# Splitting and testing feed-forward weights on GpSimd inside the attention batches, three chunks of gates ahead of the feed-forward layers, and more bias copies by VectorE in the last batch

## The chip, the cores and the metric

One core of one Trainium2 chip. The metric is the time of the device in microseconds (us); the kernel before takes 326.47 us, the median of 3 runs (325.59 to 327.27).

## The reference, cut to what matters

A transformer block on x of 8 batches x 256 tokens x 128, all in float32: an attention with 16 heads of 8 and a bias that depends on the relative position, then a gated feed-forward part with a hidden size of 512.

```python
def attn(x):                      # x: 8 x 256 x 128
    q, k, v = split(x @ W_qkv + b_qkv)                    # 16 heads of 8
    scores = einsum('bihd,bjhd->bhij', q, k) / sqrt(8) + bias[rel]
    out = einsum('bhij,bjhd->bihd', softmax(scores), v)
    return out @ W_out + b_out
def ffn(x):                       # tlin(x, w, s) = (x @ w.T) * s
    h = silu(tlin(x, w1, s1)) * tlin(x, w2, s2)           # 128 -> 512, "gate"
    h = gelu(tlin(h, h1, s1h))                            # 512 -> 512, "layer 1"
    h = gelu(tlin(h, h2, s2h))                            # 512 -> 512, "layer 2"
    return tlin(h, w3, s3)                                # 512 -> 128, "layer 3"
x = x + layernorm(attn(layernorm(x)))
x = x + layernorm(ffn(layernorm(x)))
```

## The kernel before, in words

Five engines each run a program of their own, written out by hand in the order of the work; `wait_ge` and `then_inc` on semaphores are all that ties them together. An engine takes its instructions in order, so a wait holds back all that is behind it.

**Numbers.** float32 products are made of two halves: a value is rounded to the `float32r` type that TensorE multiplies fast (the "high" part), and the rest (the "low" part) is kept beside it. So each activation of the feed-forward part is cast (ScalarE, L994 and L1028) and subtracted (GpSimd L544 or VectorE L767, L776), and `product` (L1335, L1336) multiplies the high weights with the high and the low part. The weights themselves are split too: `w_hi` and `w_lo`, 5632 columns, in 11 pieces of 512. If every low weight is zero (here the weights are -1, 0 or 1), the program takes the branch `ffn(exact=True)` with two matmuls per product; if not, the other with four. The test for that is part of the kernel: a maximum over each piece (L714), one over the eleven (L756), a transposition on TensorE (L1329), a maximum of the row (L758), and `value_load` and `If` on TensorE.

**Attention.** Batches 0 to 7, each with 8 pairs of heads (`s` = 0 to 7). While the scores of batch b are computed, TensorE also computes those of batch b+1 for their maxima (L1144, L1154), which VectorE takes (L643); the last batch has none of that. A pair's scores (L1180) are added in PSUM to its position bias, which is copied there before by ScalarE (`write_bias`, L923) or by VectorE (L650, pairs 2 and 5), or is added by TensorE (L1191, pair 7). ScalarE takes the exponential (L916), TensorE multiplies with v (`weighted`, L1204). Three PSUM tiles take turns for the scores, so the bias of pair i waits in the last batch for the exponential of pair i-3. In batch b the steps behind the attention of batch b-1 are mixed in: `back`, `weigh`, `heads_T`, `project`, `attn_moments`, `residual`, `second_norm`, `norm_T`, `keep_zT` and `z_low`. GpSimd computes the inverse deviations (`inv_std`, L503), two for each batch, and little else.

**In the last batch** ScalarE casts the weights' eleven pieces (`weights_high`, L941, `HIGH_AT`), GpSimd subtracts seven of them (L536), VectorE four (L711), and VectorE takes all the maxima.

**Feed-forward.** Four chunks of 512 tokens. `gate(c, k)` makes one of four outputs of chunk c in two PSUM banks (`GBANK`, two pairs of banks that alternate); ScalarE takes the SiLU (L1000), VectorE the product (L785). `layer1`, `layer2` give four outputs each, 8 matmuls an output, with a GELU on ScalarE (L1026); `layer3` goes back to 128. The order on TensorE is written out in `ffn`:

```python
whole(gate, 0); back(7, 0); gates 1.0, 1.1; layer1(0) with gates 1.2, 1.3; heads_T; layer1(1)
project; layer2(0); norm_T(7); gates 2.0, 2.1; layer2(1) with gates 2.2, 2.3
layer3(0); gates 3.0, 3.1; tokens_back(0); layer1(2) with gates 3.2, 3.3; layer3(1); layer1(3) ...
```

ScalarE's order is `gates(0)`, `gates(1)`, `layer(0, 0)`, `keep_onT`, `layer(1, 0)`, `layer(0, 1)`, `keep_zT`, `gates(2)`, `layer(1, 1)`, `keep_y3T(0)`, `gates(3)`, ... (its second argument is 0 for layer 1 and 1 for layer 2). SiLU and GELU need different tables, and going from one to the other inserts a table load. `A1_BANK`, `A2_BANK`, `G_SLOT` and their like say which bank and which buffer each output has, and the `free` tables in `layer1` and `layer2` what TensorE has to wait for.

## Time and profile before

| what | value |
|---|---|
| time, median of 3 runs | 326.47 us (325.59 to 327.27) |
| time of the profiled execution | 327.04 us |
| its span, first to last instruction | 325.2 us |
| busy: TensorE, VectorE, ScalarE, GpSimd | 283.9, 217.7, 212.3, 45.2 us |
| mean granted TensorE clock | 0.900 |
| first product of the feed-forward part | 215.46 us |

The span is 1.84 us shorter than that execution's time. Times in the rows are counted from the span's first instruction. "PE" is TensorE's matmuls, "PEld" its weight loads, "DVE" VectorE, "ACT" ScalarE, "POOL" GpSimd. A row's bracket says how long the engine sat idle before it, and what released it. The granted clock is a share of 2.4 GHz: 0.50 is 1.2 GHz.

### The profile page before, as it was taken

To read this page: it belongs to the slowest core of one execution; us is meant where nothing else is said; L and a number is where in the kernel's file an instruction comes from. 1 tells how busy PE (TensorE), PEld (TensorE's weight loads), DVE (VectorE), ACT (ScalarE), POOL (GpSimd) and SP (SyncE) were. 2 spreads that over 40 slices of the span, in tenths; PEclk is the share of its full clock that TensorE was granted. 3 is DMA by queue.
4 is the path that set the end of the run, shared out by engine and by line. 5 is a ranking of instruction groups with operands and counts; after the bars stand their busy time and mean duration, and the time that the engine had idled before them with its cause. 6 is when DMAs were issued, how large, how long until landed. Compare 5 with 4: busy or idle time off the path is not lost.

```text
span 325.2 us, 5036 instructions
## 1 busy us (share of the span) xinstructions
PE 283.9 (87%) x1844; PEld 186.9 (57%) x1844; DVE 217.7 (67%) x451; ACT 212.3 (65%) x313; POOL 45.2 (14%) x52
## 2 busy tenths in 40 slices
PE   8859699989999999999999966789997979699980
PEld 7644363646565555555555533346885758488870
DVE  3855355888789788897888956936558343554485
ACT  2431246678786787857878599547796576767750
POOL 3200400000001001010010137203202110300111
PEclk9985558999999999999999997559999798989997
DMA  6889800533031254522212000000000000010012
GB/s 160 260 248 245 283 2 24 183 109 100 27 89 54 67 194 171 174 87 67 78 31 62 1 3 0 1 0 2 1 2 0 0 0 0 2 32 0 1 35 69
DMA packets 22748, 23.29 MB, mean 72 GB/s; under 512 B 3745, under 2 KB 19905, under 8 KB 22465
## 3 DMA queue, kind: packets, MB, share of 16 engines
q1 hardware_dynamic: 21872, 22.38, 23.5%
q10 hardware_dynamic: 848, 0.54, 0.6%
q8 instruction: 17, 0.28, 0.4%
q14 instruction: 11, 0.08, 0.1%
HBM read 15.93 MB, written 6.68 MB: 70 GB/s over the span
## 4 chain that ended last, share of the span: by engine, by line
PE 52%; DVE 16%; ACT 11%; DMA 8%; issue 6%; SPq 4%; POOL 1%; ACTq 0%; POOLq 0%
PE place L1335 9%; PE place L1336 9%; PE place L1154 8%; PE pv L1204 7%; DVE mx L643 6%; ACT ring L916 5%; PE place L1144 4%; PE place L1180 3%; SPq L429 3%; DMA raw<-ext 2%; PE pv L1335 2%; DVE stats L569 2%; PE pv L1336 2%; DMA k_first<-z_parts 2%; DMA k_parts<-z_parts 2%
## 5 line engine op out<-in xcount | busy, mean ns | idle before, releaser
L643 DVE TENSOR_REDUCE mx<-place 128x4 f32<-128x1024 f32 x64 | 78.3, 1223 | 26.9 <-PE place L1154 25.7
L916 ACT ACTIVATE ring<-place 128x1024 f32<-128x1024 f32 x64 | 65.6, 1026 | 7.8 <-PE place L1191 5.7
L1154 PE MATMUL place<-room,identr 128*128 128x512 f32 x128 | 52.2, 492 | 3.6 <-ACT room L882 3.1
L923 ACT COPY place<-raw 128x1024 f32<-128x1024 f32 x40 | 40.8, 1021 | 16.0 <-DVE mx L643 16.0
L503 POOL TENSOR_TENSOR rstd<-mv,mhalf 128x2 f32<-128x2 f32 (+1 forms) x26 | 21.5, 827 | 205.4 <-DVE mv L577 205.4
L1335 PE MATMUL place<-room,w_hi 128*128 128x512 f32 (+1 forms) x108 | 42.6, 397 | 3.6 <-ACT ring L1026 2.9
L1336 PE MATMUL place<-room,w_hi 128*128 128x512 f32 (+1 forms) x108 | 41.9, 391 | 0.0
L1204 PE MATMUL pv<-ring,vx 128*9 128x256 f32 x512 | 37.0, 411 | 2.0 <-ACT ring L916 1.9
L1144 PE MATMUL place<-room 33*128 33x256 f32 x256 | 31.3, 325 | 8.4 <-ACT ring L916 4.0
L1180 PE MATMUL place<-room 33*128 33x256 f32 x256 | 34.2, 348 | 4.8 <-ACT place L923 3.3
L767 DVE TENSOR_TENSOR room<-ring,room 128x512 fp32r<-128x512 f32 x32 | 21.9, 691 | 22.7 <-ACT room L1028 22.7
L1180 PEld LDWEIGHTS place<-room 33*128 33x128 f32 x256 | 20.6, 198 | 21.3 <-issue 17.0
L1144 PEld LDWEIGHTS place<-room 33*128 33x128 f32 x256 | 22.1, 207 | 16.4 <-issue 13.4
L1154 PEld LDWEIGHTS place<-room,identr 128*128 128x128 f32 x128 | 21.3, 209 | 13.4 <-ACT room L882 3.7
L1335 PEld LDWEIGHTS place<-room,w_hi 128*128 128x128 f32 x108 | 20.8, 192 | 8.3 <-ACT ring L1026 3.3
L785 DVE SCALAR_TENSOR_TENSOR ring<-place,hs,raw 128x512 f32<-128x512 f32 x16 | 11.8, 750 | 20.2 <-ACT raw L1000 20.2
L928 ACT COPY oT<-pv 128x256 f32<-128x256 f32 x32 | 11.8, 369 | 19.7 <-PE pv L1204 19.7
L1204 PEld LDWEIGHTS pv<-ring,vx 128*9 128x9 f32 x512 | 11.3, 93 | 21.4 <-issue 10.0
L1336 PEld LDWEIGHTS place<-room,w_hi 128*128 128x128 f32 x108 | 20.9, 193 | 4.0
L1026 ACT ACTIVATE ring<-place,hs 128x512 f32<-128x512 f32 x25 | 17.2, 688 | 8.3 <-PE place L1336 8.3
L1028 ACT CAST room<-ring 128x512 fp32r<-128x512 f32 x32 | 19.8, 620 | 1.0
L650 DVE COPY place<-raw 128x1024 f32<-128x1024 f32 x16 | 19.6, 1226 | 0.6
(129 smaller groups left out, 395.7 us busy)
## 6 DMA issues: line engine op xcount, KB each, us to landing
raw<-ext SPq DMA_DIRECT2D x8, 384.0 KB, 7.3
room<-q_parts SPq DMA_DIRECT2D x48, 64.0 KB
room<-k_parts SPq DMA_DIRECT2D x48, 64.0 KB
w_lo<-h SPq DMA_DIRECT2D x2, 1024.0 KB, 5.0
q_parts<-w_hi SPq DMA_DIRECT2D x4, 256.0 KB, 3.1
k_parts<-w_hi SPq DMA_DIRECT2D x2, 512.0 KB, 3.4
xs<-x SPq DMA_DIRECT2D x3, 256.0 KB, 6.3
w_lo<-w SPq DMA_DIRECT2D x3, 256.0 KB, 2.8
```

What stands on the lines that cost most here:

```text
L503: nc.gpsimd.tensor_tensor(rstd[:, at:at + width], mv[:, at:at + width, 1], mhalf[:, 0:width], ALU.pow).then_inc(rstd_set, 1)
L643: nc.vector.tensor_reduce(mx[:, s // RPAIRS, :, :, s % RPAIRS].rearrange("p i k -> p k i"), max_tile(b * PAIRS + s)[:, :, :].rearrange("p ...
L767: nc.vector.tensor_tensor(lo, act_f[:, half[c], k, :], hi.bitcast(F32), ALU.subtract).then_inc((a1_lo_set, a2_lo_set)[i], 1)
L916: nc.scalar.activation(probs[:, s % PRING, :, :, :].rearrange("p k j n -> p (k j n)"), score_tile(b * PAIRS + s)[:, :, :].rearrange("p k n ...
L923: nc.scalar.copy(score_tile(i)[:, :, :].rearrange("p k (j n) -> p k j n", j=2), pair_windows(raw[:, :, :], i % PAIRS)).then_inc(bias_set, 1)
L1028: nc.scalar.copy(parts_of(slot[c], k)[0], tile).then_inc(hi_set, 1)
L1144: mm(max_tile(b * PAIRS + s)[:, half, it * S:(it + 1) * S], rows(q_rows, b, half, s)[:, it * P:(it + 1) * P], rows(k_rows, b, half, s), st ...
L1154: last = mm(max_tile(b * PAIRS + s)[:, half, :], identr[:, :], windows(table_hi[:, 2 * s + half, :], 0, P, 2, S), start=False, stop=True, ...
L1180: last = mm(tile[:, half, j * S:(j + 1) * S], rows(k_rows, b, half, s)[:, j * P:(j + 1) * P], rows(q_rows, b, half, s), start=(s in BY_PE ...
L1204: last = mm(pv[32 * r:32 * r + VC, 0:S], vx[:, b * TPB + j, 4 * g + r, :], probs[:, (2 * g + r // 2) % PRING, r % 2, j, :], start=(j == 0) ...
L1335: mm(o, w, hi, start=first, stop=False)
L1336: done = mm(o, w, lo, start=False, stop=last and exact)
```

## The change

The casts, subtractions and tests of the weights' pieces go to GpSimd, spread over batches 1 to 5 behind the second inverse deviation of each (`SPLIT_AT`: none, 1, 1, 2, 4 and 3 pieces in batches 0 to 5). A piece is now a cast, a subtraction, a comparison of the low part with zero, and a product into `w_low_all_0`; VectorE reduces that once (`largest_low`, at `s` = 3 of the last batch), TensorE turns it behind `project`, and VectorE takes the row (`any_low`, at `s` = 4). VectorE writes the last batch's biases of pairs 1, 2, 4, 5 and 6. The transposition `norm_T(6)`, `keep_zT(6)` and `z_low(6)` move into the feed-forward part. There the gates of chunks 0 to 2 come first, with the outputs of `layer1(0)` between the later ones; GpSimd casts the even outputs of the gates as well as subtracting them; two table loads are issued by hand ahead of their use.

```diff
 BY_PE = (7,)
 BY_DVE = (2, 5)
+LAST_BY_DVE = (1, 2, 4, 5, 6)
...
-        HIGH_AT = ((0, 1, 2), (3, 4), (5, 6), (7, 8), (9, 10), (), (), ())
-        LOW_AT = ((), (0,), (1,), (2, 3), (7, 4), (8, 5), (9, 6), (10,))
-        POOL_PIECES = 7
+        SPLIT_AT = ((), (0,), (1,), (2, 3), (4, 5, 6, 7), (8, 9, 10), (), ())
...
-        BY_ACT = tuple(s for s in range(PAIRS) if s not in BY_PE + BY_DVE)
+        def by_dve(b):
+            return BY_DVE if b + 1 < B else LAST_BY_DVE
+        def by_act(b):
+            return tuple(s for s in range(PAIRS) if s not in BY_PE + by_dve(b))
+        def biases_by(by, b, s):
+            return sum(len(by(n)) for n in range(b)) + sum(i <= s for i in by(b))
...
-            for b in range(B - 2):
-                inv_std(b * 2 + NU + 1, TPB)
-                inv_std(b * 2 + NU + 2, TPB)
...
+            def split_weights(piece):
+                pool.wait_ge(ffn_w_in[matrix_of(piece)], 16)
+                if piece * WPIECE < 4 * CH:
+                    pool.wait_ge(parts_out[3], PARTS_OUT)
+                elif piece * WPIECE < 8 * CH:
+                    pool.wait_ge(parts_out[4], PARTS_OUT)
+                if piece == 0:
+                    pool.wait_ge(xnT_ready, NU)
+                    nc.gpsimd.memset(w_low_all_0, 1.0).then_inc(w_low_all_0_set, 1)
+                if piece + 1 == WPIECES:
+                    pool.wait_ge(w_low_all_0_set, piece + 1)
                 cols = slice(piece * WPIECE, (piece + 1) * WPIECE)
+                nc.gpsimd.tensor_copy(w_hi[:, cols], w_lo[:, cols]).then_inc(w_hi_set, 1)
                 pool.wait_ge(w_hi_set, piece + 1)
                 nc.gpsimd.tensor_tensor(w_lo[:, cols], w_lo[:, cols], w_hi[:, cols].bitcast(F32),
                                         ALU.subtract).then_inc(w_lo_set, 1)
-            def gate_low(c):
+                pool.wait_ge(w_lo_set, piece + 1)
+                pool.wait_ge(w_low_all_0_set, piece + 1)
+                last = piece + 1 == WPIECES
+                if last:
+                    pool.wait_ge(v_ready, NU)
+                is_0 = xT[:, :] if last else w_hi[:, WCOLS - WPIECE:WCOLS]
+                nc.gpsimd.tensor_scalar(is_0, w_lo[:, cols], 0.0, None, ALU.is_equal).then_inc(w_low_is_0_set, 1)
+                pool.wait_ge(w_low_is_0_set, piece + 1)
+                nc.gpsimd.tensor_tensor(w_low_all_0, w_low_all_0, is_0 if last else is_0.bitcast(F32),
+                                        ALU.mult).then_inc(w_low_all_0_set, 1)
+            for b in range(B):
+                if b > 0:
+                    inv_std((b - 1) * 2 + NU + 1, TPB)
+                    inv_std((b - 1) * 2 + NU + 2, TPB)
+                for piece in SPLIT_AT[b]:
+                    split_weights(piece)
...
+            def gate_parts(c):
                 for k in range(0, NK, 2):
-                    pool.wait_ge(g_hi_act, c * NK + k + 1)
+                    pool.wait_ge(gate_set, c * NK + k + 1)
                     hi, lo = parts_of(G_SLOT[c], k)
+                    nc.gpsimd.tensor_copy(hi, act_f[:, G_HALF[c], k, :]).then_inc(g_hi_pool, 1)
+                    pool.wait_ge(g_hi_pool, c * (NK // 2) + k // 2 + 1)
                     nc.gpsimd.tensor_tensor(lo, act_f[:, G_HALF[c], k, :], hi.bitcast(F32),
                                             ALU.subtract).then_inc(g_lo_pool, 1)
-            for piece in range(POOL_PIECES):
-                weights_low(piece)
-            inv_std((B - 2) * 2 + NU + 1, TPB)
-            inv_std((B - 2) * 2 + NU + 2, TPB)
-            gate_low(0)
-            gate_low(1)
+            gate_parts(0)
+            gate_parts(1)
+            gate_parts(2)
             inv_std((B - 1) * 2 + NU + 1, TPB)
             inv_std((B - 1) * 2 + NU + 2, TPB)
-            gate_low(2)
-            gate_low(3)
+            gate_parts(3)
...
-            def weights_low(piece):
...
+            def largest_low():
+                dve.wait_ge(w_low_all_0_set, WPIECES + 1)
+                nc.vector.tensor_reduce(w_low_top[:, :], w_low_all_0, AX.X, ALU.min).then_inc(w_low_top_set, 1)
+                dve.wait_ge(w_low_top_set, 1)
+                nc.vector.tensor_scalar(w_low_top[:, :], w_low_top[:, :], 0.0, None,
+                                        ALU.is_equal).then_inc(w_low_top_set, 1)
+            def any_low():
+                dve.wait_ge(w_low_row, 1)
+                nc.vector.tensor_reduce(w_low_any[:, :], misc[0:1, 0:P], AX.X, ALU.max).then_inc(w_low_any_set, 1)
...
                     if b + 1 < B:
                         maxima(b + 1, s)
-                    else:
-                        for piece in LOW_AT[s]:
-                            weights_low(piece)
-                    if s + 2 in BY_DVE:
+                    if b + 1 == B and s + 1 in by_dve(b) and s == 0:
+                        write_bias(b * PAIRS + s + 1)
+                    if s + 2 in by_dve(b):
                         if b == 0:
                             dve.wait_ge(raw_in[s + 2], 16)
                         write_bias(b * PAIRS + s + 2)
...
                     if b > 0:
                         if s in (1, 2):
                             weigh(b - 1, s - 1)
+                        if s == 3 and b + 1 == B:
+                            largest_low()
                         if s == 4:
                             attn_moments(b - 1)
+                            if b + 1 == B:
+                                any_low()
...
-                        if s == 7:
+                        if s == 7 and b + 1 < B:
                             z_low(b - 1)
-            dve.wait_ge(w_low_max_set, WPIECES)
-            nc.vector.tensor_reduce(w_low_top[:, :], w_low_max[:, :], AX.X, ALU.max).then_inc(w_low_top_set, 1)
-            dve.wait_ge(w_low_row, 1)
...
+            def gate_product(c, k):
+                dve.wait_ge(silu_done, c * NK + (k + 1))
+                if c == 2:
+                    wait_gate_low(dve, 0, k)
+                elif c == 3:
+                    dve.wait_ge(a2_lo_set, k + 1)
+                nc.vector.scalar_tensor_tensor(
+                    out=act_f[:, G_HALF[c], k, :], in0=bank[GBANK[k % 2][1]], scalar=hs[:, 1, k:k + 1],
+                    in1=gate[:, k % 2, :], op0=ALU.mult, op1=ALU.mult).then_inc(gate_set, 1)
...
+            def gate_low(c, k):
+                dve.wait_ge(g_hi_act, c * (NK // 2) + k // 2 + 1)
+                hi, lo = parts_of(G_SLOT[c], k)
+                nc.vector.tensor_tensor(lo, act_f[:, G_HALF[c], k, :], hi.bitcast(F32),
+                                        ALU.subtract).then_inc(g_lo_dve, 1)
+            gate_product(0, 0)
+            gate_product(0, 1)
+            gate_product(0, 2)
+            gate_low(0, 1)
+            gate_product(0, 3)
+            gate_product(1, 0)
+            gate_low(0, 3)
+            z_low(B - 2)
+            gate_product(1, 1)
+            gate_product(1, 2)
+            gate_low(1, 1)
             weigh(B - 1, 0)
-            gates(1)
+            gate_product(1, 3)
+            gate_product(2, 0)
+            gate_low(1, 3)
+            gate_product(2, 1)
             weigh(B - 1, 1)
+            gate_product(2, 2)
+            gate_low(2, 1)
+            gate_product(2, 3)
+            gate_low(2, 3)
             layer_low(0, 0)
-            layer_low(1, 0)
             attn_moments(B - 1)
-            layer_low(0, 1, (0, 1))
+            layer_low(1, 0, (0, 1))
             residual(B - 1)
-            layer_low(0, 1, (2, 3))
+            layer_low(1, 0, (2, 3))
             second_norm(B - 1)
+            layer_low(0, 1)
+            layer_low(1, 1, (0, 1))
             z_low(B - 1)
-            gates(2)
-            layer_low(1, 1)
-            gates(3)
+            layer_low(1, 1, (2, 3))
+            gate_product(3, 0)
+            gate_product(3, 1)
+            gate_product(3, 2)
+            gate_low(3, 1)
+            gate_product(3, 3)
+            gate_low(3, 3)
...
                     ahead = b * PAIRS + s + 1
-                    if ahead < B * PAIRS and ahead % PAIRS in BY_ACT:
+                    if ahead < B * PAIRS and ahead % PAIRS in by_act(ahead // PAIRS):
                         write_bias(ahead)
...
-                    if b + 1 == B:
-                        if s == 0:
-                            act.wait_ge(parts_out[3], PARTS_OUT)
-                            act.wait_ge(parts_out[4], PARTS_OUT)
-                        for piece in HIGH_AT[s]:
-                            weights_high(piece)
-            keep_zT(B - 2)
             keep_weighted(B - 1, GROUPS - 1)
...
-            gates(0)
-            gates(1)
-            layer(0, 0)
+            def table_ahead(function):
+                nc.scalar.activation(table_loaded[:, :], mhalf[:, 0:1], function)
+            for n in range(3 * NK):
+                if n == NK:
+                    keep_zT(B - 2)
+                gate_silu(n // NK, n % NK)
+                if n % 2 == 0 and n > 0:
+                    gate_high((n - 1) // NK, (n - 1) % NK)
+            gate_high(2, NK - 1)
+            layer(0, 0, (0, 1))
             keep_onT(B - 1)
+            layer(0, 0, (2, 3))
             layer(1, 0)
             layer(0, 1)
+            layer(1, 1, (0,))
             keep_zT(B - 1)
-            gates(2)
-            layer(1, 1)
+            layer(1, 1, (1, 2, 3))
+            table_ahead(ACT.Silu)
+            gate_silu(3, 0)
+            gate_silu(3, 1)
             keep_y3T(0)
-            gates(3)
+            gate_silu(3, 2)
+            gate_high(3, 1)
+            gate_silu(3, 3)
+            gate_high(3, 3)
+            table_ahead(ACT.Gelu)
             keep_y3(0, first=True)
...
+                            if not more:
+                                pe.wait_ge(y_read, b)
+                                pe.wait_ge(w_low_top_set, 2)
+                                mm(misc[0:1, 0:P], w_low_top[:, :], ident[:, :], start=True,
+                                   stop=True).then_inc(w_low_row, 1)
...
-            pe.wait_ge(y_read, B - 1)
-            norm_T(B - 2)
             weighted(B - 1, GROUPS - 1)
...
-            pe.wait_ge(w_low_top_set, 1)
-            pe.wait_ge(exp_done, B * PAIRS)
-            mm(bank[0][0:1, 0:P], w_low_top[:, :], ident[:, :], start=True, stop=True).then_inc(w_low_row, 1)
...
-                if c == 2 and k < 2:
-                    pe.wait_ge(a1_set, (5, 7)[k])
+                if c == 3 and k < 2:
+                    pe.wait_ge(a2_set, (4, 6)[k])
...
             def ffn(exact):
-                whole(gate, 0, exact)
+                whole(gate, 0, exact, (0, 1, 2))
+                norm_T(B - 2)
+                gate(0, 3, exact)
+                whole(gate, 1, exact, (0, 1))
+                gate(1, 2, exact)
+                layer1(0, 0, exact)
                 pe.wait_ge(z_lo_set, B - 1)
                 back(B - 1, 0)
-                whole(gate, 1, exact, (0, 1))
-                with_gates(layer1, 0, 1, exact)
+                gate(1, 3, exact)
+                gate(2, 0, exact)
+                layer1(0, 1, exact)
+                back(B - 1, 1)
+                whole(gate, 2, exact, (1, 2))
+                layer1(0, 2, exact)
+                gate(2, 3, exact)
                 heads_T(B - 1)
-                whole(layer1, 1, exact)
+                layer1(0, 3, exact)
+                whole(layer1, 1, exact, (0, 1))
                 project(B - 1)
+                whole(layer1, 1, exact, (2, 3))
                 whole(layer2, 0, exact)
+                layer2(1, 0, exact)
                 pe.wait_ge(y_read, B)
                 norm_T(B - 1)
-                whole(gate, 2, exact, (0, 1))
-                with_gates(layer2, 1, 2, exact)
+                whole(layer2, 1, exact, (1, 2, 3))
                 pe.wait_ge(z_hi_set, B)
                 pe.wait_ge(z_lo_set, B)
                 layer3(0, exact, first=True)
                 whole(gate, 3, exact, (0, 1))
+                layer1(2, 0, exact)
                 tokens_back(0)
-                with_gates(layer1, 2, 3, exact)
+                whole(gate, 3, exact, (2, 3))
+                whole(layer1, 2, exact, (1, 2, 3))
                 layer3(1, exact)
                 whole(layer1, 3, exact)
```

## Rows read from the trace of the kernel before

**Rows 1.** The page's part 2, granted TensorE clock in 40 slices, tenths.

```profile
PEclk9985558999999999999999997559999798989997
```

**Rows 2.** Stretches: engine busy us (instructions), then PEclk, DMA share, GB/s.

```profile
80.00:180.00 100.00, 95.74 (x831) 56.50 (x832) 84.18 (x153) 75.16 (x106) 6.98 (x10) 1.00 0.30 91
...
188.41:196.00 7.59, 4.99 (x54) 2.53 (x54) 3.87 (x7) 7.59 (x13) 3.53 (x3) 1.00 0.01 3
...
196.00:199.30 3.30, 0.91 (x7) 0.50 (x6) 2.95 (x5) 3.30 (x6) 3.30 (x4) 0.91 0.00 0
...
199.30:215.46 16.16, 12.88 (x77) 6.00 (x77) 11.40 (x31) 10.66 (x17) 3.99 (x4) 0.50 0.00 1
...
283.90:287.20 3.30, 3.28 (x8) 2.60 (x9) 2.29 (x6) 3.03 (x5) 0.94 (x1) 0.52 0.00 0
```

**Rows 3.** Timeline of the last attention batch: start, length, engine, line.

```profile
191.78 1.65 ACT L941 CAST w_hi<-w_lo 128x512 fp32r<-128x512 f32 x3
...
192.47 8.68 POOL L536 TENSOR_TENSOR w_lo<-w_lo,w_hi 128x512 f32<-128x512 f32 x7 [5.58 <-ACT w_hi L941]
...
199.58 0.79 PE L1180 MATMUL place<-room 33*128 33x256 f32 x4 [2.38 <-ACT place L923]
...
211.42 0.66 PE L1235 MATMUL misc<-ident,y_and_z 128*128 128x128 f32 x2 [0.98 <-DVE y_and_z L580]
...
214.35 0.28 DVE L758 TENSOR_REDUCE w_low_any<-place 1x1 f32<-1x128 f32 x1 [1.33 <-PE place L1329]
...
215.46 0.79 PE L1335 MATMUL place<-z_parts,w_hi 128*128 128x512 f32 x1 [1.15 <-DVE w_low_any L758]
```

**Rows 4.** Timeline of TensorE in the feed-forward part.

```profile
241.73 0.61 PE L1228 MATMUL misc<-wo_sb,onT 128*128 128x128 f32 x4
...
249.01 0.39 PE L1335 MATMUL place<-room,w_hi 128*128 128x512 f32 x1
...
249.24 0.39 PE L1336 MATMUL place<-room,w_hi 128*128 128x512 f32 x1
...
252.39 0.41 PE L1235 MATMUL misc<-ident,y_and_z 128*128 128x128 f32 x2 [2.76 <-DVE y_and_z L580]
...
265.89 0.50 PE L1335 MATMUL pv<-room,w_hi 128*128 128x512 f32 x1 [2.40 <-ACT ring L1026]
...
283.92 0.74 PE L1335 MATMUL place<-room,w_hi 128*128 128x512 f32 x1 [2.89 <-ACT ring L1026]
```

**Rows 5.** Groups by line of ScalarE, VectorE, GpSimd: count, busy, mean ns, idle before.

```profile
L916 ACT ACTIVATE ring<-place 128x1024 f32<-128x1024 f32 x64 | 65.6, 1026 | 7.8 <-PE place L1191 5.7 <-PE place L1180 1.6
...
L923 ACT COPY place<-raw 128x1024 f32<-128x1024 f32 x40 | 40.8, 1021 | 16.0 <-DVE mx L643 16.0
...
L928 ACT COPY oT<-pv 128x256 f32<-128x256 f32 x32 | 11.8, 369 | 19.7 <-PE pv L1204 19.7
...
L1000 ACT ACTIVATE raw<-place,hs 128x512 f32<-128x512 f32 x16 | 10.9, 688 | 11.9 <-PE place L1336 11.8
...
L1026 ACT ACT_TABLE_LOAD x3 | 3.8, 1283 | 0.1
...
L785 DVE SCALAR_TENSOR_TENSOR ring<-place,hs,raw 128x512 f32<-128x512 f32 x16 | 11.8, 750 | 20.2 <-ACT raw L1000 20.2
...
L511 POOL CAST room<-raw 128x768 fp32r<-128x768 f32 x2 | 1.7, 828 | 20.8 <-DMA raw<-ext 20.8
```

**Rows 6.** Timeline of GpSimd and VectorE at several places.

```profile
163.12 0.70 POOL L503 TENSOR_TENSOR rstd<-mv,mhalf 128x2 f32<-128x2 f32 x1 [17.06 <-DVE mv L577]
...
198.09 1.22 DVE L650 COPY place<-raw 128x1024 f32<-128x1024 f32 x1
...
221.84 0.68 DVE L776 TENSOR_TENSOR room<-ring,room 128x512 fp32r<-128x512 f32 x1
...
223.30 1.28 POOL L544 TENSOR_TENSOR room<-ring,room 128x512 fp32r<-128x512 f32 x1 [1.47 <-ACT room L994]
...
224.19 0.94 DVE L776 TENSOR_TENSOR room<-ring,room 128x512 fp32r<-128x512 f32 x1 [0.69 <-ACT room L994]
```

119 lines of the change are left out of this document (33 added, 86 removed).

## The prediction

> **What bounds the kernel now.** I read the page's slices first: the granted clock of TensorE is full until about slice 24 and falls below 8 tenths for a while there, just where the last attention batch ends [rows 1]. The table of stretches says how much that matters [rows 2]. From 80 to 180 us, five attention batches, TensorE is busy 95.7% at full clock and VectorE 84.2%: little to win. In the last batch, which starts at 188.41, TensorE is busy 4.99 of 7.59 us, then 0.91 of 3.30, and from 199.3 to 215.46 the clock is 0.50, that is 1.2 GHz.
>
> The timeline of that batch [rows 3] tells why. ScalarE casts eleven pieces of feed-forward weights (L941) between its exponentials, GpSimd subtracts seven of them, and the scores of a pair wait 2.38 us for a bias that ScalarE copies late. VectorE tests the pieces, so batch 6's second norm and its transposition come at 211.42; behind them stand the last `weighted`, the test's maximum (L758) and the branch, and the first product follows at 215.46.
>
> In the feed-forward part TensorE's own timeline shows three stalls [rows 4]: 2.76 us behind the second norm, 2.40 and 2.89 behind ScalarE, which at those two places loads a table (1.28 us [rows 5]) ahead of the output that TensorE waits for. The third is followed by eight matmuls at a clock of 0.52 [rows 2], the others alike. At full clock a 512-column matmul has a pitch of 0.23 us (249.01 to 249.24), so eight at half clock lose 8 x 0.2 = 1.6 us. The tail behind the last product is untouched by the change.
>
> **Part 1: the last batch.** ScalarE loses the eleven casts and three biases (pairs 1, 4, 6) and keeps pair 3's. VectorE loses its eleven maxima, four subtractions and the late z_low, and gains those three biases at 1.22 [rows 6] and three small operations for the test. I count the batch anew from 188.41, each engine in its own order, by the durations of [rows 5] less 0.06 where operations follow each other, and 0.08 for a handover. ScalarE starts the first exponential at 189.45. It has eight at 0.96, one bias at 0.96 and six small copies at 0.31 (L928 and its like): 10.5 us. Its waits: 0.95 for pair 1, since VectorE now writes two biases in a row; 2.5 for pair 5, since the test's new `mm` stands in front of those scores on TensorE and wants `y_read`, which VectorE reaches only behind three biases and the test's minimum; 0.3 for a copy; 1.2 for pair 7, whose bias TensorE adds. The last exponential ends at 189.45 + 10.5 + 4.95 = 204.9, `weighted` takes 1.1, and the branch 0.8 (L758 ends at 214.63, the first product starts at 215.46 [rows 3]). That is 206.8 in place of 215.46: **-8.6**. The same count over the old order gives 215.4 against 215.46 measured. It stands at full clock.
>
> **Part 2: the stalls.** The 2.76 goes: from `project` (241.73) to the transposition (252.39) the vector path took 10.7 us [rows 4]. Now two outputs of layer1(1), four of layer2(0) and one of layer2(1) stand between them, 7 x 8 x 0.2275 = 12.7 us of cover. The 2.40 goes: chunk 2's gates and their table are no longer in front of chunk 1's layer-2 outputs on ScalarE, which needs an activation of 0.69 [rows 5] and a shorter cast per output, under 1.4, against TensorE's 8 x 0.2275 = 1.82. The 2.89 goes: of six table loads two fall away, and chunk 3's two are issued ahead of the wait for TensorE instead of behind it. Together 8.05, **-8.1**; with no stall over 2 us left, the three slow stretches go too, 3 x 1.6: **-4.8**. The first eight products stay at half clock, as before.
>
> New waits: two pairs of banks serve the gates, so two gates cost TensorE's 0.91, the tail of its last matmul, a SiLU of 0.69 and a product of 0.75 [rows 5] and three handovers, 2.7 us, and the first seven gates have next to no layer work among them. By count they wait 1.28, 0.68, 0.47 and 0.44, and `project` waits 0.88 for ScalarE, which now takes its first GELU outputs ahead of `keep_onT`: 3.75 against 1.85 by the same count before. The transposition moved in adds 0.2: **+2.1**. GpSimd also casts half the gates of each chunk itself, at 0.6 (L511: 0.83 for 768 columns [rows 5]), in place of ScalarE; layer 1 starts seven gates later than the first of them, which covers it.
>
> **Part 3: the split on GpSimd.** A piece is a cast (0.6), a subtraction (1.28 [rows 6]), a comparison and a product (1.28). No row has a comparison on GpSimd. Its ends are the one-input cast, 0.6, and the two-input 1.28; I take 0.6, the form with as many inputs. With the waits a piece is 3.8 us, at the upper end 4.9, and eleven are 42 us. Batch 4's four take 15.2 us in a gap of 17.06 between two inverse deviations [rows 6], so `residual` is on time; at the upper end it is 2.5 us late, once. No DMA moves, and a batch or more lies between a matrix's load and its piece.
>
> What the split can hold is VectorE. Where a VectorE subtraction with two SBUF inputs starts (224.19) inside a GpSimd operation (223.30 + 1.28 = 224.58), it takes 0.94, not 0.68 (221.84), and ends 0.55 after GpSimd does; a bias copy beside a busy GpSimd keeps its 1.22 (198.09) [rows 6]. So it is a wait for the other's end, of some forms only. In batches 1 to 5 the exposed operations are the two normalizations of `second_norm`, released by the very inverse deviation behind which the pieces stand. No row shows this form beside GpSimd. A batch loses nothing, or the rest of the cast and a whole subtraction, 0.3 + 1.3 = 1.6. VectorE idles 3.2 us per batch [rows 2] and takes up some: I take 0.3 x 5 = **+1.5**, with ends 0 and 8.
>
> A rule speaks for the upper end. The Trainium skill (SBUF — State Buffer, "Who interferes with whom") has the shared port pair as an exclusive lock for a whole instruction between GpSimd and VectorE operations with two SBUF inputs or in a two-port mode, and VectorE: DVE Perf Modes (the tier table) has an fp32 `tensor_scalar` in SBUF in such a mode. By that rule, with which the 0.55 agrees, the normalizations are held too, and the sum would carry its upper end.
>
> **Sum**, against the profiled execution's own 327.04 (span 325.2): -8.6 - 8.1 - 4.8 + 2.1 + 1.5 = -17.9, hence 309.1. The median of the runs, 326.47, lies 0.57 below that execution: **308.6 us**.
>
> **Rivals.** (a) VectorE is held at `second_norm` in every batch: 8 in place of 1.5, 315. For it: the 0.94; against it: VectorE's idle time. Chance 0.17. (b) The last batch stays at 1.2 GHz: by count TensorE is busy some 70% there, with waits of 1.4 us; 66% from 188.41 kept the clock and 28% behind it lost it [rows 2]. Then scores and `weighted` double and the gates start 4 us later: 312.6. Chance 0.15. (c) The gates starve: with more gates ahead of the layers each waits as the first do and a slow stretch follows, so that little but part 1 is won: 318. Chance 0.06. (d) The change doesn't bring the test forward: the pieces are not done by batch 7's fourth pair, the branch waits as now, and gates and layers trade stalls: within 1.6 us of 326.5. It needs pieces of over twice 3.8 us. Chance 0.03. (e) Slower: GpSimd holds VectorE in any form, maxima too. Its 42 us exceed VectorE's 15.8 idle us between 80 and 180 [rows 2] by 26: 307 + 26 = 333. It decides once each of 44 operations costs the path over 0.45 us; the unchanged 1.22 speaks against it. Chance 0.03.
>
> **Numbers.** The forecast has 0.56. The low end is no hold of VectorE (-1.5) and 3 us less for the test's wait and the gates' slow start: 304. The high end is (c), or (a) with most of (b): 318. A measurement of this kernel can tell 0.5%, 1.6 us, from no change. Faster by more: the forecast, (a), (b), (c), 0.94; same: (d), 0.03; slower: (e), 0.03.
>
> **What would show it.** The first product near 206.8; the batch behind 188.4 at clock 1.00; no wait of TensorE over 1.5 us from there until the last layer; four table loads behind the batch, not six; a GpSimd busy near 82 us; batches 1 to 6 at their old length within 0.5 us, or longer with stretched normalizations under (a). The prediction is wrong if batches grow by over 1.5 us each, or if gates wait 2 us each.

## The result and the profile after

The changed kernel takes 312.39 us (median of 4 runs, 309.96 to 314.84) against 326.63 for the kernel before (4 runs): a ratio of 0.954, 95% interval 0.944 to 0.964, so it is faster. The forecast was 308.6. Of ten runs of this kernel (these four and six later ones), seven took 308.4 to 311.4 us, at a mean granted clock of 0.936 to 0.942, and three took 314.5 to 315.2, at 0.914 to 0.916, so the median of the four falls in between. The profiled execution took 310.33 us, span 308.4, against 327.04 and 325.2 before.

From the page: part 1, and the clock of part 2, which answers to [rows 1].

```profile
PE 273.0 (89%) x1844; PEld 180.3 (58%) x1844; DVE 215.8 (70%) x440; ACT 196.9 (64%) x291; POOL 94.8 (31%) x98
...
PEclk9995555999999999999999799999999999999996
```

The hole at the end of the last batch is gone, and a small new one has come in batch 5 (one slice at 7). GpSimd is busy 94.8 us, against 45.2; I had said 82.

I cut each trace at five places that it shows clearly: the first inverse deviations of batches 1, 5 and 6 (GpSimd), the first feed-forward product (TensorE), and the end. What lies between them, in us:

| kernel | start to b1 | b1 to b5 | b5 to b6 | b6 to first product | to the end | span |
|---|---|---|---|---|---|---|
| before | 80.29 | 82.83 | 19.97 | 32.37 | 109.74 | 325.2 |
| changed | 81.67 | 85.34 | 21.54 | 22.00 | 97.85 | 308.4 |
| difference | +1.4 | +2.5 | +1.6 | -10.4 | -11.9 | -16.8 |

The first column shows no effect of the change that can be told: in the thirteen traces of this study it lies between 78.3 and 82.0, and in one of them that has the old attention part untouched it is 81.5. **When a span is compared, some 2 us of it are this start.** The other four columns repeat within 0.5 us wherever the code of a stretch is the same, the two middle ones within 0.1, and the readings below rest on them. The exception is the last column where what stands in front of it differs (e3 and e4, read below).

Stretches of the changed kernel, columns as in [rows 2]: five batches, a piece of batch 5, the last batch in two parts, and the feed-forward part in two.

```profile
80.00:180.00 100.00, 93.15 (x795) 54.48 (x794) 86.24 (x152) 71.40 (x101) 53.59 (x51) 0.98 0.31 92
174.00:177.00 3.00, 3.00 (x21) 0.98 (x20) 1.81 (x3) 1.76 (x2) 2.83 (x4) 0.52 0.30 82
188.00:200.00 12.00, 10.95 (x102) 5.85 (x102) 10.61 (x23) 9.13 (x15) 1.43 (x2) 1.00 0.01 3
200.00:210.55 10.55, 7.52 (x80) 3.72 (x79) 7.41 (x23) 6.21 (x10) 1.40 (x2) 1.00 0.00 0
...
225.00:240.00 15.00, 14.30 (x69) 11.52 (x68) 7.67 (x13) 10.07 (x17) 4.69 (x5) 1.00 0.00 1
240.00:280.00 40.00, 40.00 (x181) 33.04 (x180) 24.93 (x58) 33.17 (x55) 7.35 (x7) 1.00 0.03 7
```

The last batch keeps the full clock with TensorE 91% and then 71% busy, and from 240 to 280 TensorE never pauses: the stalls of 2.40 and 2.89 us of [rows 4] are gone. TensorE's timeline of the last batch and of the gates (answers to [rows 3] and [rows 4]):

```profile
203.91 0.38 PE L1327 MATMUL misc<-ident,w_low_top 128*1 128x128 f32 x2 [0.79 <-DVE y_and_z L700]
205.84 1.05 PE L1244 MATMUL pv<-ring,vx 128*9 128x256 f32 x16 [0.88 <-ACT ring L960]
209.57 1.05 PE L1244 MATMUL pv<-ring,vx 128*9 128x256 f32 x16 [1.11 <-ACT ring L960]
214.42 0.50 PE L1374 MATMUL place<-z_parts,w_hi 128*128 128x512 f32 x1 [1.73 <-DVE ring L804]
238.50 0.71 PE L1268 MATMUL misc<-wo_sb,onT 128*128 128x128 f32 x4 [0.69 <-ACT onT L976]
```

These are waits of under 1.8 us, where [rows 3] and [rows 4] had 2.4 to 2.9. The price stands earlier. GpSimd's groups, by shape, and then its timeline at the end of batch 4's four pieces:

```profile
L558 POOL TENSOR_SCALAR w_hi<-w_lo 128x512 fp32r<-128x512 f32 x10 | 15.0, 1504 | 0.9
L509 POOL TENSOR_TENSOR rstd<-mv,mhalf 128x2 f32<-128x2 f32 x20 | 14.9, 744 | 96.6 <-DVE mv L606 96.6
L550 POOL TENSOR_TENSOR w_lo<-w_lo,w_hi 128x512 f32<-128x512 f32 x11 | 14.1, 1285 | 0.9
L560 POOL TENSOR_TENSOR xn<-xn,w_hi 128x512 f32<-128x512 f32 x10 | 12.8, 1284 | 0.8
...
L548 POOL CAST w_hi<-w_lo 128x512 fp32r<-128x512 f32 x11 | 6.8, 616 | 0.1
```

```profile
147.44 0.61 POOL L548 CAST w_hi<-w_lo 128x512 fp32r<-128x512 f32 x1
...
165.78 1.28 POOL L560 TENSOR_TENSOR xn<-xn,w_hi 128x512 f32<-128x512 f32 x1
167.01 0.73 POOL L509 TENSOR_TENSOR rstd<-mv,mhalf 128x2 f32<-128x2 f32 x1
...
170.58 0.61 POOL L548 CAST w_hi<-w_lo 128x512 fp32r<-128x512 f32 x1
171.28 1.27 POOL L550 TENSOR_TENSOR w_lo<-w_lo,w_hi 128x512 f32<-128x512 f32 x1
```

The comparison takes 1.50 us. I had bounded it by 0.6 and 1.28, so a piece takes 4.9 us where I took 3.8, and the inverse deviation at 167.01 has no idle time before it: it stands behind batch 4's last product, where in [rows 6] GpSimd had been idle for 17.06 us. VectorE and then TensorE at the same place:

```profile
164.26 0.56 DVE L606 TENSOR_SCALAR mv<-mv 128x2 f32<-128x2 f32 x1
164.74 1.21 DVE L672 TENSOR_REDUCE mx<-place 128x4 f32<-128x1024 f32 x1
167.78 0.60 DVE L609 TENSOR_SCALAR y_and_z<-y_and_z,mv,rstd 128x128 f32<-128x128 f32 x2 [1.82 <-POOL rstd L509]
...
170.88 1.74 DVE L609 TENSOR_SCALAR y_and_z<-xs,mv,rstd 128x128 f32<-128x128 f32 x2
```

```profile
172.77 0.41 PE L1275 MATMUL misc<-ident,y_and_z 128*128 128x128 f32 x2 [3.34 <-DVE y_and_z L609]
```

The values for the inverse deviation were ready at 164.82 (164.26 + 0.56), so it comes 2.2 us late. The step that makes them ready, L606, is itself longer: 0.56 us beside GpSimd's comparison, 0.17 in every other batch, which is 0.4 of the +2.5. The second norm then runs into batch 5's first pieces: its pair of normalizations takes 1.74 us, against 0.60 for the pair at 167.78, which ran beside no piece, and ends at 172.62, just behind the subtraction (171.28 + 1.27 = 172.55). TensorE stands 3.34 us, and the clock is 0.52 from 174 to 177. By these rows that is where the +2.5 and the +1.6 come from; e1 and e2 below test it.

Such a held pair takes 1.77 us in batches 2, 3 and 4 as well (0.89 in batch 1), and yet batches 1 to 3 are as long as before (20.35, 20.84 and 20.81 us from the first inverse deviation of each batch to that of the next; before 20.35, 20.82 and 20.80). Batch 4 is too in e1, which has the hold without the overrun (20.84; before 20.86). ScalarE's table loads, which answer to [rows 5]:

```profile
L1070 ACT ACT_TABLE_LOAD x2 | 2.6, 1283 | 0.0
...
L1020 ACT ACT_TABLE_LOAD x1 | 1.3, 1283 | 0.0
L1049 ACT ACT_TABLE_LOAD x1 | 1.3, 1283 | 0.0
```

Four in the feed-forward part, where there were six.

### The profile page after: what moved, and what is told of

Same layout as the page of the kernel before. It is cut to its first block, busy times and chain, and to the rows that moved or that the text cites. A ratio compares the mean times of both kernels' runs of the same rounds, so it can differ in the third digit from the quotient of the medians.

```text
span 308.4 us, 5066 instructions
## 1 busy us (share of the span) xinstructions
PE 273.0 (89%) x1844; PEld 180.3 (58%) x1844; DVE 215.8 (70%) x440; ACT 196.9 (64%) x291; POOL 94.8 (31%) x98
## 4 chain that ended last, share of the span: by engine, by line
PE 47%; DVE 18%; ACT 9%; POOL 7%; DMA 7%; issue 6%; SPq 5%; ACTq 0%; POOLq 0%; DVEq 0%
PE place L1374 9%; PE place L1375 9%; PE place L1194 6%; DVE mx L672 5%; PE pv L1244 5%; ACT ring L960 4%; PE place L1220 3%; PE place L1184 3%; SPq L435 3%; DMA raw<-ext 3%; DVE y_and_z L609 2%; DVE stats L598 2%; POOL w_hi L558 2%; PE place L1117 2%; DMA k_first<-z_parts 2%
## 5 line engine op out<-in xcount | busy, mean ns | idle before, releaser
L967 ACT COPY place<-raw 128x1024 f32<-128x1024 f32 x37 | 37.8, 1020 | 18.9 <-DVE mx L672 18.9
L1374 PE MATMUL place<-room,w_hi 128*128 128x512 f32 (+1 forms) x116 | 44.7, 387 | 0.7 <-DVE room L792 0.7
L1375 PE MATMUL place<-room,w_hi 128*128 128x512 f32 (+1 forms) x116 | 44.1, 383 | 0.0
L1244 PE MATMUL pv<-ring,vx 128*9 128x256 f32 x512 | 35.3, 395 | 2.4 <-ACT ring L960 2.3
L1184 PE MATMUL place<-room 33*128 33x256 f32 x256 | 30.6, 319 | 6.4 <-DMA room<-k_first 3.5
L1220 PE MATMUL place<-room 33*128 33x256 f32 x256 | 32.8, 337 | 2.0 <-DMA room<-mrow 1.3
L1220 PEld LDWEIGHTS place<-room 33*128 33x128 f32 x256 | 19.6, 190 | 18.5 <-issue 14.3
L1184 PEld LDWEIGHTS place<-room 33*128 33x128 f32 x256 | 21.7, 204 | 13.5 <-issue 9.0
L1194 PEld LDWEIGHTS place<-room,identr 128*128 128x128 f32 x128 | 21.2, 209 | 14.2 <-ACT room L926 5.1
L1374 PEld LDWEIGHTS place<-room,w_hi 128*128 128x128 f32 x116 | 21.8, 188 | 5.1 <-DVE room L792 0.9
L1375 PEld LDWEIGHTS place<-room,w_hi 128*128 128x128 f32 x116 | 21.8, 188 | 4.2
L679 DVE COPY place<-raw 128x1024 f32<-128x1024 f32 x19 | 23.2, 1225 | 0.6
L804 DVE SCALAR_TENSOR_TENSOR ring<-place,hs,raw 128x512 f32<-128x512 f32 x16 | 11.9, 748 | 15.2 <-ACT raw L1028 15.1
L1049 ACT ACTIVATE ring<-place,hs 128x512 f32<-128x512 f32 x27 | 18.5, 686 | 5.9 <-PE place L1375 5.9
```

The lines of the kernel that those rows point to most:

```text
L679: nc.vector.tensor_copy(score_tile(i)[:, :, :].rearrange("p k (j n) -> p k j n", j=2), pair_windows(raw[:, :, :], i % PAIRS)).then_inc(bia ...
L967: nc.scalar.copy(score_tile(i)[:, :, :].rearrange("p k (j n) -> p k j n", j=2), pair_windows(raw[:, :, :], i % PAIRS)).then_inc(bias_set, 1)
L1184: mm(max_tile(b * PAIRS + s)[:, half, it * S:(it + 1) * S], rows(q_rows, b, half, s)[:, it * P:(it + 1) * P], rows(k_rows, b, half, s), st ...
L1194: last = mm(max_tile(b * PAIRS + s)[:, half, :], identr[:, :], windows(table_hi[:, 2 * s + half, :], 0, P, 2, S), start=False, stop=True, ...
L1220: last = mm(tile[:, half, j * S:(j + 1) * S], rows(k_rows, b, half, s)[:, j * P:(j + 1) * P], rows(q_rows, b, half, s), start=(s in BY_PE ...
L1244: last = mm(pv[32 * r:32 * r + VC, 0:S], vx[:, b * TPB + j, 4 * g + r, :], probs[:, (2 * g + r // 2) % PRING, r % 2, j, :], start=(j == 0) ...
```

## The experiments

**Theory A**: the time above the best of this order is batch 4's overrun (four pieces of 4.9 us in a gap of 17.06) and the slow stretch that follows. **Theory B**: it is the hold of VectorE at the second norm. Later a third question came up: what makes the last batch lose its clock.

The stretches of all the experiments' traces, and their ratios to the kernel before:

| kernel | to b1 | b1 to b5 | b5 to b6 | b6 to first product | to the end | span | ratio (95%) |
|---|---|---|---|---|---|---|---|
| e5 (changed, again) | 81.25 | 85.27 | 21.49 | 22.00 | 98.1 | 308.1 | 0.952 (0.947 to 0.956) |
| e3 attention only | 78.29 | 85.31 | 21.50 | 22.07 | 107.4 | 314.6 | 0.977 (0.971 to 0.984) |
| e4 feed-forward only | 81.48 | 82.89 | 19.97 | 31.27 | 96.6 | 312.2 | 0.962 (0.957 to 0.967) |
| e1 even | 80.28 | 82.81 | 20.20 | 22.78 | 98.0 | 304.1 | 0.942 (0.937 to 0.947) |
| e2 sum | 79.09 | 82.82 | 20.20 | 21.82 | 98.0 | 301.9 | 0.932 (0.927 to 0.938) |
| e6 e1, behind norm | 80.69 | 82.89 | 19.96 | 26.62 | 98.2 | 308.4 | 0.949 (0.944 to 0.954) |
| e7 e1, test later | 79.55 | 82.82 | 20.21 | 21.61 | 97.9 | 302.1 | 0.937 (0.932 to 0.941) |
| e8 e6 and e7 | 81.55 | 82.88 | 19.97 | 24.57 | 98.3 | 307.3 | 0.938 (0.932 to 0.944) |
| e9 early, norm, later | 79.90 | 82.85 | 19.95 | 20.83 | 98.3 | 301.8 | 0.933 (0.929 to 0.937) |
| e10 early, later | 82.03 | 82.86 | 20.20 | 21.23 | 97.8 | 304.1 | 0.935 (0.931 to 0.939) |
| e11 e1, biases | 79.90 | 82.89 | 20.18 | 23.25 | 97.9 | 304.1 | 0.942 (0.938 to 0.947) |

**e1, an even split.** One piece fewer in batch 4, so that none outlasts the next inverse deviation's due time; two pieces go to batch 6.

```diff
-        SPLIT_AT = ((), (0,), (1,), (2, 3), (4, 5, 6, 7), (8, 9, 10), (), ())
+        SPLIT_AT = ((), (0,), (1,), (2, 3), (4, 5, 6), (7, 8), (9, 10), ())
```

> The same pieces, spread one to two batches later: 1, 1, 2, 3, 2 and 2 in batches 1 to 6, so that no batch has over three (14.7 us of GpSimd in a gap of 17). Theory A (the four pieces of batch 4 overran their gap, held the inverse deviation by 2.5 us, and the stall dropped the clock once, 1.5 us): some 4 us less than the changed kernel, 308 against 312 by the medians, batches 4 to 6 at 20.8 us each, GpSimd busy as before at 95 us. Theory B (VectorE is slowed by every GpSimd piece, the second norms above all): the same eleven pieces cost the same, the time moves by less than 1 us.

Measured 307.0 us (305.99 to 307.56), where 308 was expected. The stretch b1 to b5 is back at its old 82.81 and b5 to b6 at 20.20; no slice behind the first ones is slow. The hold is still there. TensorE and VectorE of e1 at the same place, the second norm in batch 5:

```profile
169.05 0.41 PE L1275 MATMUL misc<-ident,y_and_z 128*128 128x128 f32 x2 [1.06 <-DVE y_and_z L609]
```

```profile
167.16 1.74 DVE L609 TENSOR_SCALAR y_and_z<-xs,mv,rstd 128x128 f32<-128x128 f32 x2
```

The held pair costs TensorE 1.06 us of waiting and the batch only 0.23 (20.20 against 19.97). So theory A carries the difference: 3.9 us in the two stretches, of which 0.8 is given back in the last batch (22.78 against 22.00), where two pieces now end close before the test and its matmul waits 1.18 us, not 0.79.

**e2, a cheaper test.** The changed kernel, with the comparison and the product replaced by one addition of the low part to the sum; this leaves out the sound test of the weights (low parts of opposite sign can cancel).

```diff
-                nc.gpsimd.tensor_scalar(is_0, w_lo[:, cols], 0.0, None, ALU.is_equal).then_inc(w_low_is_0_set, 1)
-                pool.wait_ge(w_low_is_0_set, piece + 1)
-                nc.gpsimd.tensor_tensor(w_low_all_0, w_low_all_0, is_0 if last else is_0.bitcast(F32),
-                                        ALU.mult).then_inc(w_low_all_0_set, 1)
+                nc.gpsimd.tensor_tensor(w_low_all_0, w_low_all_0, w_lo[:, cols], ALU.add).then_inc(w_low_all_0_set, 1)
```

> Pieces where the change has them, but the comparison (1.50 us each) and the product are replaced by one addition of the low part to a running sum; this leaves out a sound test (low parts that cancel would be missed). A piece is 3.3 us in place of 4.9. Theory A: four of them are 13.2 us and fit the gap, so as much is gained as by the even spread, 308. Theory B: held time falls with the number of GpSimd operations, from four to three a piece, so a quarter of the loss, about 1 us.

Measured 303.55 us (303.33 to 305.0), where 308 was expected; of the 3.4 below e1, 1.0 stands in the last batch (no piece falls in batch 6) and 1.2 in the start. Four pieces of 3.3 us fit batch 4's gap, and both stretches are those of e1: the changed kernel's own split, with a short enough piece, has no overrun. It shows theory A from the other side, by the length of a piece and not by their number.

**e3 and e4, one half of the change each.** e3 has the new attention part and the old order of the feed-forward part, e4 the reverse; the last batch's second-norm transposition goes with the feed-forward order. e3's diff against the changed kernel, at its core (banks, slots and the orders of the other engines follow it); e4's, against the kernel before, is the same order put in.

```diff
-                whole(gate, 0, exact, (0, 1, 2))
-                norm_T(B - 2)
-                gate(0, 3, exact)
...
+                whole(gate, 0, exact)
...
+                whole(gate, 1, exact, (0, 1))
+                with_gates(layer1, 0, 1, exact)
...
+                whole(gate, 2, exact, (0, 1))
+                with_gates(layer2, 1, 2, exact)
```

> The split on GpSimd, its test and the last batch's biases as in the change; the feed-forward part in the order of before, with the transposition of batch 6's norm back in front of the last weighted sum. The forecast's terms give -8.6 + 1.5 = 319.5; with what the changed kernel's trace shows (last batch 10.0 shorter, batches 4 to 6 4.1 longer) 326.6 - 5.9 = 320.7. Rival (the gain of the last batch exists only together with the moved transposition, since the last weighted sum waits for the second norm again): 323 or more.

> The feed-forward part as in the change, its casts of gates on GpSimd too; the weights split and tested in the last batch by three engines as before, VectorE's biases as before. The forecast's terms for the stalls are -8.1 - 4.8 + 2.1 = -10.8: 315.8; the changed kernel's trace gives -12.2: 314.4. Rival (the new order only looked good because the gates started at full clock behind a dense batch): under half of it, above 320.

Measured 318.84 us (316.93 to 324.16) and 314.0 (312.73 to 314.09). By the stretches the two halves don't overlap in the middle: e3 has the changed kernel's batches and last batch (22.07), e4 its feed-forward part (96.6) behind the old last batch. In e3 the three stalls are back, to the hundredth:

```profile
243.47 0.30 PE L1247 MATMUL misc<-ident,y_and_z 128*128 128x128 f32 x1 [2.76 <-DVE y_and_z L607]
...
255.39 0.50 PE L1348 MATMUL pv<-room,w_hi 128*128 128x512 f32 x1 [2.40 <-ACT ring L1038]
...
273.39 0.80 PE L1348 MATMUL place<-room,w_hi 128*128 128x512 f32 x1 [2.89 <-ACT ring L1038]
```

But e3's feed-forward part is 107.4 long, not 109.7. It starts at full clock. Its first 2.5 us beside those of before, in which six products were issued, not twelve; e3's row first, then that of the kernel before:

```profile
207.17:209.70 2.53, 2.12 (x12) 1.43 (x8) 0.00 (x0) 2.36 (x5) 0.00 (x0) 1.00 0.00 0
```

```profile
215.46:218.00 2.54, 2.54 (x6) 2.06 (x7) 0.00 (x0) 0.77 (x3) 0.00 (x0) 0.50 0.00 0
```

That start is worth only 0.6 us: from the first product to the transposition behind the stall of 2.76 e3 takes 36.3 us, the kernel before 36.9. The larger part, 1.6 us, comes behind that stall. The clock fell after it before the change and did not in e3, though the wait is the same, 2.76 us; again e3's row first:

```profile
243.47:247.00 3.53, 3.53 (x17) 2.95 (x18) 1.10 (x3) 2.92 (x4) 0.00 (x0) 1.00 0.00 0
```

```profile
252.39:256.00 3.61, 3.61 (x12) 2.87 (x13) 1.18 (x2) 2.61 (x4) 0.00 (x0) 0.62 0.00 0
```

In e4 the new order alone is worth 13.1 us in the feed-forward part and 1.1 in the last batch. The spans' gains, 10.6 and 13.0, add to 6.8 more than 16.8. Of that the starts are 2.2. The last batch is 1.0: what the new order takes out of it (the transposition, `keep_zT` and `z_low`) goes with 1.1 us there beside the old split and with nothing beside the new one (22.07 in e3, 22.00 in the changed kernel). The feed-forward part is the remaining 3.5. There e3 has 2.3, read above, that don't add to the new order's gain, and e4, which starts at full clock too (1.00 from 215.61 to 218), is 1.3 shorter than the changed kernel. 1.0 of that stands at the first gates: ScalarE loads its table from 213.95 in e4, before the first product (215.61), and from 211.08 in the changed kernel, behind it (210.55), so the wait of 1.73 us there is 0.78 in e4:

```profile
218.49 0.50 PE L1377 MATMUL place<-z_parts,w_hi 128*128 128x512 f32 x1 [0.78 <-DVE ring L797]
```

**e5, the changed kernel again**, to see what its runs spread over.

> The changed kernel itself again. Its runs lay at 310 (granted clock 0.937) and at 314.6 (0.915), the kernels without an overrun of batch 4 within 1.7 us of each other. Theory A: what spreads is the price of the stall of 3.3 us near 170 us, since after it TensorE's clock is down for a stretch that differs from run to run; then both levels appear again, and a trace of the upper one has its extra slow stretch behind that stall or in the last batch. Theory C: the spread is the load phase ahead of 80 us, which differs by 3.4 us among the traces so far; then runs differ there and the clock of the rest is alike.

Measured 309.75 us (308.43 to 315.18, six runs; the kernel before 325.5 beside it). The trace repeats the rows read above (a stall of 3.32 us at 172.27, the first product at 210.01). One run of six took 315.18 at a clock of 0.916. No trace caught such a run of this kernel, so where its clock goes stays open, and neither theory is shown.

**e6, the pieces behind the norm.** e1, with each batch's pieces held until its second norm has been written, so that GpSimd can't hold the normalizations.

```diff
+                if b > 0 and SPLIT_AT[b]:
+                    pool.wait_ge(z_set, b)
                 for piece in SPLIT_AT[b]:
```

> The even spread, and each batch's pieces start only when VectorE has written the second norm. In the even spread the two normalizations wait for a GpSimd cast and a subtraction (TensorE idle 1.06 and 1.08 us at 169 and 189), and the distance between the first inverse deviations of batches 5 and 6 was 20.20 us, 19.97 before the change. Theory B' (the hold is real but costs only where the norm's transposition is next on TensorE, 0.2 us a time): the normalizations are back at 0.34 each, that distance at 19.97, and all together 0.3 to 0.6 us less. Rival (the hold costs what TensorE idles, 1 us in each of batches 5 and 6, hidden by noise of the start): over 1.5 us less.

Measured 309.27 us (307.45 to 310.33): slower than e1, against what I expected. The hold is indeed gone and b5 to b6 is 19.96, so the hold's full price in such a batch is 0.24 us. The loss is elsewhere: batch 6's two pieces start and end 1 us later (14.7 us behind that batch's first inverse deviation, 13.7 in e1), and VectorE stands before the test's minimum until then, with the read of `project`'s result (L702) behind it. VectorE and TensorE of e6, and the stretch behind the wait:

```profile
198.28 0.69 DVE L740 TENSOR_REDUCE w_low_top<-xn 128x1 f32<-128x512 f32 x1 [1.66 <-POOL xn L560]
...
200.20 0.41 DVE L702 TENSOR_TENSOR y_and_z<-misc,bo_bc 128x256 f32<-128x256 f32 x1
```

```profile
200.67 0.38 PE L1329 MATMUL misc<-ident,w_low_top 128*1 128x128 f32 x2 [2.56 <-DVE y_and_z L702]
202.59 1.90 PE L1246 MATMUL pv<-ring,vx 128*9 128x256 f32 x16 [0.89 <-ACT ring L962]
```

```profile
201.00:210.00 9.00, 7.00 (x49) 3.06 (x48) 3.27 (x15) 3.33 (x4) 1.43 (x2) 0.56 0.00 0
```

After a wait of 2.56 us the `weighted` takes 1.90 us for sixteen matmuls, not 1.05: the last batch is at 1.2 GHz again and takes 26.62 us. All four runs of e6 have a mean granted clock of 0.931 to 0.936, those of e1 0.937 to 0.942.

**e7, the test one pair later.** e1 with the test's `mm` in front of pair 6's scores in place of pair 5's, and `any_low` behind the residual.

```diff
-                            if not more:
+                        if s == 5 and not more:
                                 pe.wait_ge(y_read, b)
                                 pe.wait_ge(w_low_top_set, 2)
```

> The even spread, with the test's small matmul on TensorE one pair later, behind the scores of pair 5, and its reading on VectorE behind the residual. In the even spread TensorE waits 1.18 us in front of that matmul with the scores of pair 5 behind it. If the wait stands on the path of the last batch, as my count had it, the first feed-forward product comes 0.8 to 1.2 us earlier from the batch's first inverse deviation (22.78 us to it); if the exponential of pair 7 and VectorE's biases set the end anyhow, under 0.3 us.

Measured 304.63 us (304.04 to 304.91), the last batch at 21.61 against 22.78: -1.17, as expected. So much the wait in front of the test's `mm` cost in the even split; in the changed kernel itself, where it is 0.79 us, it was not taken out.

**e8, both.** e6 with e7's later test.

> Even spread, pieces behind the second norm and the later test together: the sum of the two, 1.1 to 1.7 us below the even spread's 307.0, hence 305.5, and below the changed kernel's 312.4 by 2.2%.

Measured 307.58 us (304.04 to 310.4), a miss. In the trace, of the run of 309.05 us, the wait is 2.11 us and the clock falls behind it:

```profile
201.52 0.38 PE L1329 MATMUL misc<-ident,w_low_top 128*1 128x128 f32 x2 [2.11 <-DVE y_and_z L702]
...
207.15 1.89 PE L1246 MATMUL pv<-ring,vx 128*9 128x256 f32 x16 [1.11 <-ACT ring L962]
```

But the four runs are not alike: 304.04 and 306.12 us have a mean granted clock of 0.946 and 0.940, 309.05 and 310.4 have 0.931 and 0.921. So the same program seems to have kept the clock in some runs, and the miss is one of those that lost it; only one of the four has a trace.

**e9 and e10, the pieces early.** Only one piece is left in batch 6. e9 has e6's wait and e7's test, e10 e7's test without the wait; e10's line is the first of this diff alone.

```diff
-        SPLIT_AT = ((), (0,), (1,), (2, 3), (4, 5, 6), (7, 8), (9, 10), ())
+        SPLIT_AT = ((), (0,), (1,), (2, 3), (4, 5, 6), (7, 8, 9), (10,), ())
...
+                if b > 0 and SPLIT_AT[b]:
+                    pool.wait_ge(z_set, b)
```

> Batch 6's split is pulled forward: its two pieces no longer fall in batch 6 (steps of three in batch 5, one in batch 6), the pieces of each batch wait until that batch's second normalization is through, and the last batch's test stands one pair later. Theory (a GpSimd piece that is under way makes the normalization late, and a late test is what made the last batch lose its clock in the version with the wait): batch 5 to 6 near 19.97 us, no TensorE gap over 1.2 us behind 160 us, the last batch at clock 1.00 and its first feed-forward product about 21.6 us behind the inverse deviation of batch 6; time near 304.0. Rival (the wait itself costs the clock, whenever the test comes): last batch at 1.2 GHz again, time near 307.5.

> The same places of the pieces and the later test, without the wait for the normalization. Theory of the hold: batch 5 to 6 back near 20.2 us with a gap of about 1 us, time near 304.6, as the version with only the later test. Rival (the places in batches 4 to 6 matter and the wait doesn't): the same time as the run beside it, within 0.2 us, and batches of equal length.

Measured 304.02 us (303.07 to 305.09) and 305.43 (303.9 to 306.04). The same wait that cost e6 and e8 their clock costs e9 nothing, since GpSimd ends its last piece at 192.34, 5.7 us ahead of the test:

```profile
191.07 1.27 POOL L560 TENSOR_TENSOR xn<-xn,xT 128x512 f32<-128x512 f32 x1
```

```profile
198.07 0.38 PE L1329 MATMUL misc<-ident,w_low_top 128*1 128x128 f32 x2 [0.36 <-DVE y_and_z L702]
...
202.55 1.05 PE L1246 MATMUL pv<-ring,vx 128*9 128x256 f32 x16 [1.11 <-ACT ring L962]
```

The rival (the wait itself costs the clock) falls; in e6 and in e8's trace the clock went with the late test. Between e9 and e10 the hold shows twice, 0.25 us in b5 to b6 and 0.4 in the last batch. The rest of the 1.4 us between their medians is not told from noise, since their traces' starts differ by 2.1 us. e9's last batch (20.83) and its b5 to b6 (19.95) are the shortest of all versions; its time beats the changed kernel's and ties with e7's.

**e11, the biases back on ScalarE.** e1 with the last batch's bias copies as they were.

```diff
-LAST_BY_DVE = (1, 2, 4, 5, 6)
+LAST_BY_DVE = (2, 5)
```

> The even split with the last batch's bias copies left as in the kernel before. Theory of the record (the last batch got shorter because its split and its stalls are gone, the copies hardly matter): first feed-forward product 0.2 us later, time near 307.2. Rival (the copies moved to VectorE are what made the last batch short: three copies of about 1 us off the queue of ScalarE): 3 us later, time near 310.

Measured 306.42 us (305.77 to 310.0), the last batch 23.25 against 22.78: the three copies moved to VectorE are worth 0.5 us where I expected 0.2, and far from 3. Most of it comes back at once: the first gates wait 1.39 us in e11 and 1.75 in e1, and the two spans are alike (304.1). That part of the change could have been left out almost for free.

## Why the prediction was right, and where it was not

The forecast was -17.9 against the profiled execution's own time, and -17.9 for the medians; measured were -16.8 between the profiled spans, and -14.2 between the medians. Of the 2.6 between these, 2.1 is how far the changed kernel's median lies above its profiled execution. Sign, range and mechanism of the terms hold.

That the sum came within 1.1 us of the profiled spans is partly luck, for the errors cancel: the last batch and part 2 gained 1.8 and 1.1 us more than counted, the split cost 2.6 more, and the start, which had no term, 1.4. Of the signs named, the full clock behind 188 and the four table loads came. The first product came at 210.55, not near 206.8; GpSimd is busy 94.8 us, not 82; one wait, of 1.73, is over 1.5; and batches 4 and 5 grew by 2.5 and 1.6, which is more than the 1.5 us given as a sign of being wrong, though only these two did. By its own steps:

- **Part 1, the last batch, -8.6.** Measured -10.4 from batch 6 to the first product. The step was right as a mechanism, the clock at 1.00 behind 188 included, and its size 1.8 too small. Two terms of the count were too large. The waits of ScalarE: 2.5 before pair 5 was 1.84, 0.95 before pair 1 was 0.64, 1.2 before pair 7 was 1.16, 1.0 us together (ScalarE's work itself, counted as 10.5, was 10.8). And the branch's 0.8, which isn't there at all: the last exponential ends at 209.51, `weighted` follows at 209.57, and the first product starts at 210.55, within it. In [rows 3] the branch waited for the test's maximum (L758), which VectorE now takes 5.8 us ahead (L745, at 204.77). e11 shows that of this term the moved biases are 0.5 us; the rest is the removed split and test, and the clock, which no run takes apart.
- **Part 2, stalls -8.1 and slow stretches -4.8.** Right: e3 has the 2.76, 2.40 and 2.89 back with the old order, and the changed kernel has none. With the new waits of +2.1 the forecast for the part is -10.8 and the measured one -11.9. The price of a slow stretch is right too: behind the stall of 2.76, e3 without one is 1.6 us shorter. The step that failed is "the first eight products stay at half clock, as before": they run at 1.00, worth 0.6 us by e3. The gates' first waits were counted as 1.28, 0.68, 0.47 and 0.44; they are 1.73, 0.43 and 0.29, and `project` waits 0.69, not 0.88: 3.1 us together where 3.75 were counted.
- **Part 3, the split, +1.5.** Measured +4.1, and the mis-sized term is the comparison. "I take 0.6, the form with as many inputs" gave 3.8 us a piece; it took 1.50 us, outside my bounds too, and a piece 4.9, just my upper end. The step named the consequence ("at the upper end it is 2.5 us late, once"): it came 2.2 late, for +2.5. The two bounds don't share one count, though: 3.8 is the four durations alone (3.76), while 4.9 has some 0.5 for handovers on top of 4.44. Start to start, a piece takes 0.2 more than its four operations, so it would have been 4.0 with a comparison of 0.6, and that 4.9 was met is in part luck. What I had not followed up is what that lateness sets off: the second norm, late by now and held like the others, makes TensorE's stall 3.34 us, and a slow stretch follows, for the other 1.6, of which the hold alone is 0.2 (e1).
- **The hold of VectorE.** The 0.3 us per batch was right where it shows (0.23 in b5 to b6), and zero in batches 1 to 4, though the normalizations are held in all of them. A normalization that meets GpSimd's subtraction, the form that no row of before showed beside GpSimd, ends 0.07 to 0.08 us after that whole instruction. The rule of the Trainium skill (SBUF — State Buffer, "Who interferes with whom", and the tier table of VectorE: DVE Perf Modes) agrees with this trace in these rows. It does not fit one other: L606 at 164.26 is stretched to 0.56 us beside the comparison, but ends 0.87 before it. Yet the price of 8 us in place of 1.5 was wrong. That VectorE's idle time takes the hold up is my reading; what the runs show is batches of the old length. Rival (a) had the mechanism right and the price wrong.
- **Rival (b), the last batch at 1.2 GHz,** did not happen in the profiled run: TensorE was busy 71% behind 200, about the 70% that the rival argued from, with waits up to 1.1 us, and kept the clock. In the traces of e6 and e8 it did happen, behind a wait of over 2 us in that batch. Such a wait doesn't bring it every time (e8's other runs, and e3's 2.76 us). Whether it is what the three longer runs of the changed kernel have, whose wait at that place is 0.79 in both traces, no trace shows.
- **The test's wait on TensorE** was priced inside part 1; taking it out is worth 1.2 us in the even split (e7).
